# Graph layer on one core: order of the last group's products and scatters, and the place of the next to last node tile, changed

## The reference

```
h = relu(layernorm(x))
xs, xv = s @ W1_s, v @ W1_v                         # per node
w = silu(edge_embed @ fc_w1 + fc_b1) @ fc_w2 + fc_b2   # per edge, 192
msg = products of w, xs[src], xv[src] and edge_sh   # 96 scalars, 96 vectors
agg = segment_sum(msg, dst)
out = agg @ W2 + h @ Wsc                            # scalars, vectors
feats = silu(out_s[:64]), out_v * silu(out_s[64:96])
result = x + h + feats
```

## Time and profile before

| | us |
|---|---|
| median of 3 runs | 541.65 |
| lowest and highest | 541.38, 541.88 |
| profiled execution, its own time | 543.1 |
| its span, from the first to the last instruction | 541.4 |
| TensorE matmul busy | 469.7 (87%) |
| VectorE busy | 352.3 (65%) |
| ScalarE busy | 202.8 (37%) |
| GpSimd busy | 394.3 (73%) |

### The profile page before, as it was taken

How to read it: one execution, slowest core, us unless ns; L and a number is a source line. 1 busy time by engine, 2 the same in 40 slices (tenths; PEclk the granted TensorE clock), 3 DMA queues, 4 the chain that set the end, 5 groups by cost and what they waited for, 6 DMA issues and landing times.

```text
span 541.4 us, 17264 instructions
## 1 busy us (share of the span) xinstructions
PE 469.7 (87%) x5423; PEld 350.1 (65%) x5423; DVE 352.3 (65%) x1234; ACT 202.8 (37%) x416; POOL 394.3 (73%) x425
## 2 busy tenths in 40 slices
PE   6739689789799989989989899899899898999996
PEld 5735556557567656766667577677567566776675
DVE  7944664765666667667557656767675676576765
ACT  4653332333333433434333333334333343345331
POOL 7746777777777777777777777777777777777770
PEclk9988798999799989989989989999899899899997
DMA  9992222323322232322223233322323332332221
GB/s 217 386 283 67 70 70 72 72 71 78 76 67 75 75 77 71 76 74 72 75 77 75 67 78 77 75 71 74 76 71 76 75 75 72 77 77 73 69 73 30
DMA packets 36231, 48.20 MB, mean 89 GB/s; under 512 B 10200, under 2 KB 28859, under 8 KB 35683
## 3 DMA queue, kind: packets, MB, share of 16 engines
q0 software_dynamic: 19776, 33.78, 24.9%
q1 hardware_dynamic: 16009, 13.98, 8.9%
q10 hardware_dynamic: 410, 0.07, 0.1%
HBM read 39.60 MB, written 4.00 MB: 81 GB/s over the span
## 4 chain that ended last, share of the span: by engine, by line
PE 40%; POOL 21%; issue 13%; DVE 11%; DMA 9%; DVEq 2%; SPq 2%; ACT 0%; POOLq 0%
POOL gath L568 21%; PE ps L866 12%; PE ps L876 7%; DMA gath<-table,src_sb 6%; PE ps L853 6%; PE ps L871 4%; DVE P L686 3%; DVE agg L724 3%; PE ps L872 2%; PE ps L908 2%; DMA dq<-dst_q 1%; DMA table<-prod 1%; DVEq L709 1%; SPq L192 1%; PE ps L859 1%
## 5 line engine op out<-in xcount | busy, mean ns | idle before, releaser
L568 POOL DMA_INDIRECT gath<-table,src_sb x388 | 368.1, 949 | 126.7 <-issue 107.0
L876 PE MATMUL ps<-S,P 128*64 128x24 f32 x2496 | 168.0, 219 | 0.0
L866 PE MATMUL ps<-fc_sb,hid 128*128 128x384 f32 x416 | 163.2, 518 | 0.0
L871 PE MATMUL ps<-S,P 128*64 128x36 f32 x832 | 117.7, 236 | 49.2 <-DVE agg L724 48.5
L876 PEld LDWEIGHTS ps<-S,P 128*64 128x64 f32 x2496 | 156.9, 140 | 0.0
L681 DVE TENSOR_TENSOR P<-ps,gath 128x512 f32<-128x512 f32 x103 | 71.1, 691 | 126.4 <-DMA gath<-table,src_sb 65.3
L871 PEld LDWEIGHTS ps<-S,P 128*64 128x64 f32 x832 | 81.1, 137 | 111.5 <-DVE agg L724 72.0
L601 ACT ACTIVATE hid<-ps,fb_sb 128x256 f32<-128x256 f32 x104 | 49.2, 473 | 186.8 <-PE ps L853 118.5
L872 PE MATMUL ps<-S,P 128*64 128x12 f32 x832 | 107.9, 207 | 0.0
L686 DVE TENSOR_TENSOR P<-ps,gath 128x384 f32<-128x384 f32 x206 | 104.1, 547 | 0.0
L866 PEld LDWEIGHTS ps<-fc_sb,hid 128*128 128x128 f32 x416 | 81.1, 205 | 34.3 <-issue 6.4
(11 more groups left out here) (119 smaller groups left out, 347.4 us busy)
## 6 DMA issues: line engine op xcount, KB each, us to landing
slow<-table SPq DMA_DIRECT2D x512, 0.6 KB
gath<-table,src_sb POOLq DMA_INDIRECT x388, 2.6
agg<-zeros SPq DMA_DIRECT2D x4, 1024.0 KB
out<-res SPq DMA_DIRECT2D x24, 78.1 KB
x_sb<-x SPq DMA_DIRECT2D x5, 350.0 KB
emb<-emb_t SPq DMA_DIRECT2D x104, 16.0 KB
table<-prod SPq DMA_DIRECT2D x3, 420.0 KB
sh_sb<-sh_t SPq DMA_DIRECT2D x1, 840.0 KB, 9.3
```

Source lines behind the costliest of these rows:

```text
L568: nc.gpsimd.indirect_dma_start(gath[:, u, j, :], None, table, bass.IndirectOffsetOnAxis(ap=src_sb[:, t:t + 1], axis=0)).then_inc(arrived, 16)
L866: ins = nc.tensor.matmul(w_ps(u)[:, 2 * g:2 * g + 2, 0:WN], hid[:, u % 2, g, :], fc2_sb[:, :, :], start=False, stop=True, skip_group_check ...
L871: nc.tensor.matmul(oj[0:64, :, 0:3], pj[:, 64:128], sj[:, :, 1:4], start=True, stop=True)
L876: ins = nc.tensor.matmul(oj[64:128, :, c:4:3 - c], pj[:, lo:lo + 64], sj[:, :, 0:2 + c:1 + c], start=(c == 0), stop=(c == NC - 1), skip_gr ...
```

## The change

VectorE issues both register loads right behind the residual of node tile 22, computes all four products of group 103 ahead of the additions of group 102, in the order 0, 1, 3, 2, and adds the windows of group 103 in that order. TensorE scatters in the same order, and node tile 23 comes behind the four scatters. The counts waited for go by the place k in the order, the tile by j. No instruction of an engine is added or left out.

```diff
--- before.py
+++ after.py
@@ -31,6 +31,7 @@
 NG = NN // G
 LEAD = 3
 EPS = 1e-5
+LAST_ORDER = (0, 1, 3, 2)
 ZEROS, ZERO_DMA = 2048, 8192
 WARM_NODES = 17
 MINB_AT = 20
@@ -724,9 +725,9 @@
                             nc.vector.tensor_tensor(a, out_ps(q)[:, j, :, :].rearrange("p n c -> p (n c)"), a,
                                                     ALU.add).then_inc(p_agg, 1)
 
-                    def last_add(j, col):
-                        dve.wait_ge(p_out, NQ + max(j, 1))
-                        dve.wait_ge(p_agg, NT - QT + j)
+                    def last_add(k, j, col):
+                        dve.wait_ge(p_out, NQ + max(k, 1))
+                        dve.wait_ge(p_agg, NT - QT + k)
                         a = agg[:, bass.ds(col, WIN * AC)]
                         nc.vector.tensor_tensor(a, last_ps(j).rearrange("p n c -> p (n c)"), a, ALU.add).then_inc(p_agg, 1)
 
@@ -805,17 +806,17 @@
                     def last(tile):
 
                         residual(tile)
+                        cols, rest = columns(NQ - 2), columns(NQ - 1)
                         last_products(0)
                         with_input(NN - 2)
                         last_products(1)
+                        last_products(3)
                         with_input(NN - 1)
-                        cols, rest = columns(NQ - 2), columns(NQ - 1)
+                        last_products(2)
                         dve.wait_ge(n_cols, NN - 1)
                         add_windows(NQ - 2, SLOTS - 2, cols, more=False)
-                        last_products(2)
-                        last_products(3)
-                        for j in range(QT):
-                            last_add(j, rest[j])
+                        for k, j in enumerate(LAST_ORDER):
+                            last_add(k, j, rest[j])
                         gated(NN - 2)
                         residual(NN - 2)
                         gated(NN - 1)
@@ -888,10 +889,10 @@
                             ins = scatter_tile(P[:, u % 2, j, :], S[:, u % 2, j, :, :], out_ps(q)[:, j, :, :])
                         ins.then_inc(p_out, 1)
 
-                    def last_scatter(j):
+                    def last_scatter(k, j):
                         u = SLOTS - 1
-                        pe.wait_ge(p_prod, NQ + j)
-                        if j == 0:
+                        pe.wait_ge(p_prod, NQ + k)
+                        if k == 0:
                             pe.wait_ge(p_S, NQ)
                         if j == 3:
                             pe.wait_ge(p_agg, NT - 2 * QT)
@@ -939,11 +940,9 @@
                     weights(NQ - 1, SLOTS - 1)
                     scatter(NQ - 2, 0)
                     own_part(o_ps[2], hT[:, NN - 1, 0, :], hT[:, NN - 1, 1, :])
-                    last_scatter(0)
-                    last_scatter(1)
+                    for k, j in enumerate(LAST_ORDER):
+                        last_scatter(k, j)
                     node_tile(NN - 2)
-                    last_scatter(2)
-                    last_scatter(3)
                     pe.wait_ge(p_agg, NT)
                     sums_part(o_ps[2], [agg_v[:, N - NTN:N, k] for k in range(AC)])
```

## The result

22 runs of each kernel: 541.93 us median before, 542.88 us changed; the ratio is 1.0018, with a 95% interval of 1.0011 to 1.0025. The change makes the kernel slower by about 0.98 us, 0.18%, just inside the 0.2% that the prediction set as no change. Forecast were +0.70 us and 542.35. One of the 22 executions of the changed kernel took 592.71 us at a mean granted clock of 0.718 and is left out of the ratio.

What follows compares the result with a forecast made beforehand. VectorE's queue of products, inputs and additions up to its last addition, then the final sums, set the end. Loads +0.57, order +0.08 and TensorE tie +0.05 give +0.70 on 541.65: 542.35 us, range 541.2 to 543.3.

Steps and rivals of the forecast that it cites:

- the rival with TensorE as the bound: End of TensorE's work: an earlier clock fall makes node tile 23 end behind VectorE's additions; 542.4 to 543.2 us, chance 0.26.
- the likeliest case: Last stretch: register loads exposed on VectorE, node tile 23 level with the last addition; 541.9 to 542.8 us, chance 0.52.
- register loads uncovered: VectorE behind tile 22's residual: two 342 ns loads hold the sequencer and delay products 0; +0.57 us, bounds 0 to 0.95.
- order of products and additions, without the stall: VectorE, groups 102 and 103: products no longer stand between the addition chains, where they covered a dependency of 0.28 us.
- the stall, 0.17 before: VectorE, between halves of products 2: out-of-line 0.17 us won back; if tied to its program place, up to 0.3 back.
- the tie on TensorE: TensorE before the final sums: node tile 23 ends at 535.8, level with VectorE's 535.76; +0.05 us added.
- the item on the order: VectorE's products, inputs and additions in the new order: 4.97 us against 4.89, +0.08, bounds -0.3 to +0.4.
- The loads hidden: VectorE's sequencer passes the register loads or gets far enough ahead; only +0.08 remains, 541.7 us, chance 0.13.
- The final sums at full clock: TensorE's final sums: clock kept until 537, so 1.02 us instead of 2.05; 541.27 us, chance 0.09.
- The loads by the other price: VectorE's register loads at the skill's floor of about 600 ns: loads about 1.1 us, whole change about +1.2.
- Slower by more than 0.2% or not: Whole kernel: chance 0.25 of being slower by over 1.08 us, 0.72 within that, 0.03 faster.

Runs made afterwards that it cites:

- e2: Kernel before, only the two register loads moved right behind node tile 22's residual; 5.95 us from that residual to the final sums, times not compared.
- e1: Changed kernel, the two register loads put back in front of group 102's additions; 5.80 us from tile 22's residual to the final sums, ratio 0.9999.
- e5: Changed kernel, register loads put back and ten memsets added in VectorE's preparation; 5.46 us from tile 22's residual to the final sums, ratio 0.9998.
- e6: Kernel before, ten memsets added in VectorE's preparation; 5.22 us from tile 22's residual to the final sums, ratio 0.9995.
- e3: Changed kernel, ten one-column memsets added at the start of VectorE's preparation; 6.07 us from tile 22's residual to the final sums, ratio 1.0022.
- e4: Changed kernel, node tile 23 put back between group 103's second and third scatters on TensorE; 6.41 us from tile 22's residual to final sums, ratio 1.0022.
- third order: Kernel before, each half of products 2 and 3 placed behind one addition of group 102; ratio 0.9989 with ten memsets, 1.0004 in a run without.
- f4: Kernel before, halves of products 2 and 3 between group 102's additions, no memsets, repeated; 4.97 us from tile 22's residual to final sums, ratio 1.0004.
- f2: Kernel before, ten memsets, product halves between group 102's additions, node tile 23 split around scatters 2 and 3; 5.05 us residual to final sums, ratio 0.9992.
- f1 again: Kernel before, ten memsets, product halves between group 102's additions, repeated on the 841 us chip; 6.18 us from tile 22's residual to final sums, ratio 0.9969.
- f3: Kernel before, product halves between group 102's additions, no memsets, on the 841 us chip; 5.76 us from tile 22's residual to final sums, ratio 0.9865.

## Why the prediction was right or wrong, point by point

The direction and the mechanism held, and the time lies in the range. That 542.88 comes near the 542.35 is in part chance of the base: the kernel before came to 541.93 in 22 executions and not to the 541.65 of three, which is 0.28 of the 0.53 missed. By its number alone 542.88 would even belong to the rival with TensorE as the bound (542.4 to 543.2) and not to the likeliest case (541.9 to 542.8); the trace decides between them. In the likeliest case's own terms, by the stretch:

| term | forecast | measured | by |
|---|---|---|---|
| register loads uncovered | +0.57 | +0.61 to +0.63 | residual to products 0 in e2; changed less e1 |
| order of products and additions, without the stall | +0.25 | +0.24 | e5 less e6 |
| the stall, 0.17 before | -0.17 | +0.19 | changed less e3 (0.36), before less e6 (0.17) |
| the tie on TensorE | +0.05 | 0 | idle for 1.11 us ahead of the final sums |
| sum | +0.70 | +1.04 | |

The first two are the sum's own steps: each load is 342 ns of the sequencer in program order, and the dependent step that products used to cover came to 0.41 against the 0.40 taken. (The pieces written down for the loads add up to 530.54 and +0.59, not to 530.52 and +0.57.)

**The term that was mis-sized** is in the item on the order: "the out-of-line 0.17 is won back". I named its bound in the same sentence, a stall tied to its place that would come back among the additions as up to 0.3, and took the other value. It came back as 0.36, a little over that bound too, and the whole item, forecast at +0.08 within -0.3 to +0.4, came to +0.43 (0.24 and 0.19). My reading is that between additions the sequencer waits for the engine each time and has handed nothing over ahead, so the stall counts in full, where between products the engine still worked off the first half meanwhile. The runs agree (0.36 and 0.35 between an address operation and its addition, 0.17 between halves, nothing in e3), but none tests it by itself. That one mis-sized term (from -0.17 to +0.19, 0.36) is the whole difference of 0.34 between forecast and measured stretch; the tie, 0.05 too much, and the loads, 0.04 too little, nearly cancel. The clue stood in the rows of before: 0.37 in place of 0.20 with no wait named.

**TensorE the bound:** it did not happen, and neither did the tie of the forecast. Node tile 23 ran behind the scatters as forecast (it starts 3.78 behind the residual; the working has 3.68), but at the upper clock level except for its last matmuls, and was done by 533.7, 0.8 us before the last addition began. TensorE's granted clock fell between 533.4 and 533.6, 0.9 us later against the residual than before:

```profile
533.20:533.40 0.20, 0.20 (x4) 0.20 (x3) 0.10 (x1) 0.00 (x0) 0.00 (x0) 1.00 0.14 41
533.40:533.60 0.20, 0.20 (x3) 0.14 (x2) 0.11 (x1) 0.00 (x0) 0.00 (x0) 0.64 0.00 0
```

e4, with the tile out of the way, has the same stretch. That the moment of the fall moves against the work was rightly left open, and that it came late enough here is luck: had the clock fallen 4.16 us behind the residual, as before, the prediction's own working (1.43 us for the tile, twice that at the lower level) has it end at 6.3 by my estimate, close to the 6.43 at which the final sums start.

**The loads hidden:** refuted by e2, where moving them is all that was done.

**The final sums at full clock:** the premise was wrong. I took their 2.05 us for the price of 1.2 GHz. In e4 the granted clock stayed at its upper level through them, and they took as long: from their start to ScalarE's gates behind them 2.06 us (535.77 to 537.83), against 2.07 before (535.11 to 537.18). TensorE over the final sums of e4 and, below it, of the kernel before (length; busy PE, PEld, DVE, ACT, POOL; granted clock, DMA):

```profile
535.70:537.80 2.10, 2.02 (x8) 1.91 (x8) 0.54 (x3) 0.00 (x0) 0.00 (x0) 1.00 0.11 28
```

```profile
535.10:537.20 2.10, 2.04 (x8) 1.90 (x8) 0.47 (x2) 0.02 (x1) 0.00 (x0) 0.50 0.12 32
```

Weight loads are busy for 1.9 us at either level. So nothing could be had from the clock there, and a rival with a chance of 0.09 had none. Beside it, the rule on activity and clock in the Trainium skill ("TensorE: Matmul & The Clock Gate", Part 1) did not enter: whatever keeps the clock up, these eight matmuls did not get faster with it.

**The loads by the other price.** The Trainium skill's floor for a register load ("DMA: Bandwidth & Descriptors", latency and other measured facts: about 600 ns) would have made the whole about +1.2, by chance near the measured 1.04. The gap in e2 (0.84 less 0.23, for two loads) agrees with the 342 ns of the rows, and not with that floor.

**Slower by more than 0.2% or not:** 0.18% with an interval up to 0.25% sits on the bound that was set, and the 0.25 given to slower was not too much. The stretch, with its 1.04, accounts for all of the 0.98 us.

## What to carry to other kernels

On an engine whose sequencer runs ahead, a register load is free only behind enough queued work: count what the engine has in hand where the load stands, and put address loads behind products, not in front. Operations that depend on each other are the place for independent work; gathering the independent work in one block and the dependent chain in another costs the cover, here 0.24 us for no wait removed. And when one step in a timeline is out of line with no wait named, look up its place in the program before assuming that a new order will be rid of it.

## What the runs showed of the hardware that was not expected

- A stall of 0.35 us or so stands at one place of VectorE's program, between numbers 22 and 23 from the residual, in three different orders of the work (before, changed, third order), and in both executions without memsets on the chip that took 841 us; with ten memsets far ahead it lies ten instructions further back. It cost 0.17 between the halves of a product, 0.36 between an address operation and its addition, and nothing where the engine had work in hand.
- The trace has a sign of what the sequencer does there. The DMA queue of kind "instruction" moves exactly one packet of 8 KB between the residual and the end in each of the 14 profiled executions. In seven of the eight without memsets it starts 0.67 or 0.68 us behind the start of number 23 (0.95 in e2); with the memsets it comes earlier, 2.4 to 2.8 us behind the residual in place of 3.7 to 4.9. That speaks for a place where one block of instructions ends and the next is begun. What the 0.35 us are spent on stays open: the packet comes after them. The line below is from the view of the DMA queues of the changed kernel, 533.2 to 533.3 (packets, MB, share of 16 engines):

```profile
q14 instruction: 1, 0.01, 27.2%
```

- The final sums, which read their weights from `agg` with a stride of four elements, take 2.02 us at 2.4 GHz and 2.04 at 1.2 GHz; the same matmuls on the contiguous copy take some 1.0 in node tile 23. The weight loads show it: 0.53 for the first two and 1.47 for the other six in e4 at 2.4 GHz and in the kernel before at 1.2 GHz, but 0.30 and 0.73 from the copy at 2.4 GHz. That the stride is the reason was not tried; the clock is ruled out.
- The moment at which the clock falls at the end of the pass differs from one execution to the next: during scatter 3 in the kernel before, behind node tile 23 in e3, and not before the end of the final sums in e1 and f4.
- Where TensorE comes late to the stretch, VectorE's order no longer decides: the first addition of group 102 then waits for that group's scatter, behind which the own part of node tile 24 follows. It starts 0.61 us behind that own part in f2 and f1 again, but 0.26 in f3 (817.84 to 818.10), which is as late and has no memsets. The 0.35 between them fits the stall: in the third order the memsets put it between the wait for that scatter and the address of the first addition. So ten instructions further back is a free place in e3 and e5 and not in every order.
